# Loading the joint pass's constants and first tiles during the second feature transform

## The reference

```python
# second graph layer: one head, 2048 -> 768
h   = h1 @ W2                                  # "second transform"
e   = leaky_relu((h @ a_src)[src] + (h @ a_dst)[dst], 0.2)
ex  = exp(e - segment_max(e, dst)[dst])
gnn = segment_sum(h[src] * (ex / segment_sum(ex, dst)[dst]), dst) + b2

# linear attention, per head (12 heads of 64, 256 random features)
dash = q * 64 ** -0.25 @ proj.T                # proj: the random map
q_p  = exp(dash - diag(q) - max(dash)) + 1e-4
out  = (q_p @ context) / (q_p @ k_sum)         # context, k_sum: sums over the keys
mix  = out @ w_proj.T + b_proj

x = x + gnn + mix
```

## Time and profile before

| | before |
|---|---|
| median of three runs | 3599.15 us (3598.68 to 3605.56) |
| profiled execution: its time, its span | 3594.7 us, 3592.9 us |
| second transform, first issue to the last store's landing | 1761.6 to 2206.3 us |
| joint pass, first issue to last store's issue | 2208.0 to 2986.5 us |
| TensorE busy over the span | 3106.6 us (86%), mean granted clock 0.926 |
| DMA, whole span | 219 GB/s |

### The profile page before, as it was taken

The page is one execution under the profiler, slowest core; times in us unless marked ns, Lnnn a source line. Parts: engine busy times, 40 slices in busy tenths (PEclk is TensorE's granted clock), DMA queues, the critical chain, the costliest instruction groups (busy, mean ns, idle before and its releaser), DMA issues. The chain is left out here.

```text
span 3592.9 us, 63295 instructions
## 1 busy us (share of the span) xinstructions
PE 3106.6 (86%) x21962; PEld 2542.8 (71%) x21963; DVE 1944.3 (54%) x4537; ACT 1125.4 (31%) x2419; POOL 1503.7 (42%) x1497
## 2 busy tenths in 40 slices
PE   7974999999999789999799995999999996589920
PEld 6973677777777568889799995666666663389920
DVE  4853667666666554444522222666666664633357
ACT  2322434343434243333412221333333322223321
POOL 1323677777777400000000002777777751233346
PEclk9997999999999899999899997899999996689965
DMA  5746788888888465544466674999999975456767
GB/s 184 235 160 198 238 264 261 269 259 264 264 268 263 129 202 139 136 136 140 171 82 86 87 88 150 352 325 327 326 326 328 327 269 192 156 198 239 237 229 255
DMA packets 275948, 786.79 MB, mean 219 GB/s; under 512 B 81326, under 2 KB 94353, under 8 KB 272438
## 3 DMA queue, kind: packets, MB, share of 16 engines
q0 software_dynamic: 96640, 416.68, 35.5%
q1 hardware_dynamic: 178998, 366.17, 34.6%
HBM read 676.48 MB, written 167.42 MB: 235 GB/s over the span
## 5 line engine op out<-in xcount | busy, mean ns | idle before, releaser
L940 POOL DMA_INDIRECT k_rows<-tab,k_pick x576 | 598.1, 1038 | 234.7 <-issue 175.1
L2161 POOL DMA_INDIRECT m_rows<-tab,m_e x500 | 490.0, 980 | 200.8 <-issue 143.4
L1400 PE MATMUL k_num<-k_rows,k_wt 128*32 128x384 f32 (+1 forms) x3200 | 283.2, 494 | 14.3 <-ACT k_wt L1032 14.3
L142 PE MATMUL g_prod<-g_w_hi,g_h_h 128*128 128x384 f32 x768 | 258.0, 336 | 3.4 <-DVE g_h_l L1766 3.4
L143 PE MATMUL g_prod<-g_w_lo,g_h_h 128*128 128x384 f32 x768 | 257.8, 336 | 0.0
L144 PE MATMUL g_prod<-g_w_hi,g_h_l 128*128 128x384 f32 x768 | 257.8, 336 | 0.0
L1661 PE MATMUL f_prod<-f_a_h,f_w_hi 128*128 128x512 f32 (+1 forms) x672 | 253.9, 378 | 2.5 <-DVE f_w_lo L1604 2.5
L1663 PE MATMUL f_prod<-f_a_h,f_w_lo 128*128 128x512 f32 (+1 forms) x672 | 246.5, 367 | 0.0
L1662 PE MATMUL f_prod<-f_a_l,f_w_hi 128*128 128x512 f32 (+1 forms) x672 | 246.4, 367 | 0.0
L1730 POOL MEMSET g_row<- 128x1 f32 x2 | 0.1, 101 | 542.3 <-issue 542.3
L1597 DVE TENSOR_TENSOR f_a_l<-f_turn,f_a_h 128x512 fp32r<-128x512 f32 (+1 forms) x168 | 98.8, 628 | 210.1 <-ACT f_a_h L1564 210.1
(11 more groups left out here) (366 smaller groups left out, 7675.5 us busy)
## 6 DMA issues: line engine op xcount, KB each, us to landing
agg<-k_outb SPq DMA_DIRECT2D x100, 384.0 KB
f_a_in<-agg SPq DMA_DIRECT2D x100, 384.0 KB, 7.3
g_h<-h SPq DMA_DIRECT2D x25, 1024.0 KB, 12.1
ys<-e_y SPq DMA_DIRECT2D x56, 384.0 KB, 2.9
h<-f_e SPq DMA_DIRECT2D x16, 1024.0 KB, 5.2
tab<-q_xn SPq DMA_DIRECT2D x25, 388.5 KB, 5.4
tab<-g_row SPq DMA_DIRECT2D x25, 385.5 KB, 4.6
m_own<-tab SPq DMA_DIRECT2D x25, 385.5 KB, 9.0
```

Of the source, the lines that this page charges most:

```text
L142: pe.matmul(out, x_hi[k], w_hi[k], start=(k == 0), stop=False)
L940: pool.indirect_dma_start(rows[:, place(u, n), :], None, dram["tab1"], at, bounds_check=bound, oob_is_err=False).then_inc(rows_in[i], 16)
L1400: mm = pe.matmul(num[i][o, 0:n], wt[u % 2][:, v, o], rows[:, place(u, 2 * (half + v) + g), a:a + n], start=(v == 0), stop=(v == 1), tile_p ...
L2161: pool.indirect_dma_start(rows[:, place(h, c) + k, :], None, tab, bass.IndirectOffsetOnAxis(ap=e[h % 4][:, 0, k * SLOTS + c:k * SLOTS + c ...
```

## The change

A new class `QueryAhead` owns, in an outer pool around both stages, the buffers and semaphores of the map, the context, the diagonal, the projection weights, the low parts of the two query tiles and the four edge-list buffers. SyncE fills them inside the second transform, right after `store(1)`, once the last weight piece has been split; these are 24 DMAs: map (2), diagonal, context, query tiles 0 and 1, projection weights (6), edge lists of tiles 0, 1 and 2 (12). The staging ring of `W2` has no buffers of its own any more: it uses those of the projection weights and so has 12 places instead of 16. In the joint pass SyncE starts with the ramp, input tile 0 and the biases; in each turn the own rows now come first, then edge lists, query tile, input tile. The outer pool ends with a barrier of its own. In the skipped variant the same class is made inside its pool.

```diff
+class QueryAhead:
+    HELD = 3
+    def fetch(self, sp):
+        for i, buf in enumerate((self.pj_h, self.pj_l)):
+            sp.dma_start(buf[:, :].bitcast(F32), self.dram["pj"][i, :, :]).then_inc(self.pj_in, 16)
+        sp.dma_start(self.diag[:, :], self.dram["mix"][:, CTXW:MIXW]).then_inc(self.diag_in, 16)
+        sp.dma_start(self.ctx[:, :], self.dram["mix"][:, 0:CTXW]).then_inc(self.ctx_in, 16)
+        for t in range(2):
+            self.load_q(sp, t)
+        for k in range(KC):
+            sp.dma_start(self.w[:, k, :], self.io["wprojT"][k * P:(k + 1) * P, :]).then_inc(self.w_in, 16)
+        for h in range(self.HELD):
+            self.load_edges(sp, h)
...
-def phase_g(nc, io, dram, keep):
+def phase_g(nc, io, dram, keep, ahead):
...
-        SR = 16
-        stage = [s.sb(f"stage{b}", [P, 384]) for b in range(SR)]
+        SR = 2 * KC
+        stage = [ahead.w[:, b // 2, 384 * (b % 2):384 * (b % 2) + 384] for b in range(SR)]
...
                 sp.dma_start(dram["ald2"][bass.ds(r, P), :], row[b][:, D + 2:D + 3]).then_inc(out_sem[b], 16)
+                if first and b == 1:
+                    sp.wait_ge(wlo_done, len(JOBS))
+                    ahead.fetch(sp)
...
-                load_q(0)
-                for i, (buf, n) in enumerate(((pj_h, 0), (pj_l, 1))):
-                    sp.dma_start(buf[:, :].bitcast(F32), dram["pj"][n, :, :]).then_inc(pj_in, 16)
-                sp.dma_start(diag[:, :], dram["mix"][:, CTXW:MIXW]).then_inc(diag_in, 16)
+                if not merged:
+                    held.fetch(sp)
                 if merged:
                     sp.dma_start(ramp[:, :], io["node_ids"][0:P].partition_broadcast(P)).then_inc(ramp_in, 16)
-                    load_edges(0)
-                sp.dma_start(ctx[:, :], dram["mix"][:, 0:CTXW]).then_inc(ctx_in, 16)
+                load_x(0)
                 sp.dma_start(bias[:, :], io["bproj"].partition_broadcast(P)).then_inc(bias_in, 16)
                 if merged:
                     sp.dma_start(att[1][:, :], io["b2"].partition_broadcast(P)).then_inc(bias_in, 16)
-                load_x(0)
-                load_q(1)
-                if merged:
-                    load_edges(1)
                 for t in range(NT + 2):
-                    if merged and t + 2 < NT:
+                    if merged and t < NT:
+                        load_own(t)
+                    if merged and QueryAhead.HELD <= t + 2 < NT:
                         load_edges(t + 2)
                     if t + 2 < NT:
                         load_q(t + 2)
                     if t + 1 < NT:
                         load_x(t + 1)
-                    if merged and t < NT:
-                        load_own(t)
-                    if t == 0:
-                        for k in range(KC):
-                            sp.dma_start(w[:, k, :], io["wprojT"][k * P:(k + 1) * P, :]).then_inc(w_in, 16)
                     if t >= 2:
                         store(t - 2)
...
-        phase_g(nc, io, dram, keep)
-        mix_out(nc, io, dram, keep, True)
-        mix_out(nc, io, dram, keep, False)
+        with Pool(nc, "a") as a:
+            ahead = QueryAhead(nc, io, dram, keep, a)
+            phase_g(nc, io, dram, keep, ahead)
+            mix_out(nc, io, dram, keep, ahead)
+        mix_out(nc, io, dram, keep, None)
```

More of the change, by code:

```diff
@@ L1746, in _ @@
                 act.wait_ge(staged[n % SR], 16 * (n // SR + 1))
-                act.activation(w_hi[:, k, o], stage[n % SR][:, :], ACT.Copy).then_inc(whi_done, 1)
+                act.activation(w_hi[:, k, o], stage[n % SR], ACT.Copy).then_inc(whi_done, 1)
             def step(p, b, first, last):
@@ L2009, in _, with mix_out @@
                 groups(pe, lambda T: None, group, lambda T, n: None)
-def mix_out(nc, io, dram, keep, merged):
+def mix_out(nc, io, dram, keep, ahead):
+    merged = ahead is not None
     GR = P // TW
@@ L2025, in mix_out @@
     with Pool(nc, "m" if merged else "c") as s:
-        pj_h, pj_l = s.sb("pj_h", [P, M], F32R), s.sb("pj_l", [P, M], F32R)
-        ctx, diag = s.sb("ctx", [P, CTXW]), s.sb("diag", [P, NT * HEADS])
-        w = s.sb("w", [P, KC, D])
-        qt_h, qt_l = s.sb2("qt_h", [P, KC, P], F32R), s.sb2("qt_l", [P, KC, P], F32R)
+        held = ahead if merged else QueryAhead(nc, io, dram, keep, s)
+        pj_h, pj_l, ctx, diag, w, qt_l = held.pj_h, held.pj_l, held.ctx, held.diag, held.w, held.qt_l
+        qt_h = s.sb2("qt_h", [P, KC, P], F32R)
         qp, qpt = s.sb("qp", [P, HEADS * M]), s.sb2("qpt", [P, 4 * P])
@@ L2046, in mix_out @@
             ramp, ones = s.sb("ramp", [P, P]), s.sb("ones", [P, P])
-            e = [s.sb(f"e{b}", [P, 2, S], I32) for b in range(4)]
+            e, e_in = held.e, held.e_in
             rows = s.sb("rows", [P, RING, TROW2])
@@ L2057, in mix_out @@
             out_b = [s.bank(f"out{i}") for i in range(2)]
-            ramp_in, e_in = s.sem("ramp_in"), [s.sem(f"e_in{b}") for b in range(4)]
+            ramp_in = s.sem("ramp_in")
             ald_in, own_in, rows_in = s.sem2("ald_in"), s.sem2("own_in"), keep["rows_in"][1]
@@ L2081, in load_q @@
                         sp.wait_ge(dash_full, 6 * (t - 1))
[L2082 to L2083 removed]
+                    held.load_q(sp, t)
                 def load_x(t):
@@ L2092, in load_edges @@
                         sp.wait_ge(z1_done, h - 3)
-                    for k in range(GR):
-                        lo = sp.value_load(keep["ranges"][0:1, 2 * (GR * h + k):2 * (GR * h + k) + 1], min_val=0, max_val=EP)
-                        sp.dma_start(e[h % 4][:, :, k * SLOTS:(k + 1) * SLOTS],
-                                     io["edges"][:, bass.ds(lo, CAP)].rearrange("s (p c) -> p s c", c=SLOTS)).then_inc(e_in[h % 4], 16)
+                    held.load_edges(sp, h)
                 def load_own(h):
```

27 lines of the change are left out of this document (21 added, 6 removed).

## The result

| | before | changed |
|---|---|---|
| median, runs side by side | 3600.30 us (3598.68 to 3605.56) | 3662.54 us (3660.39 to 3663.52) |
| ratio, 95% interval | | 1.0169 [1.0152, 1.0187] |
| profiled execution: time, span | 3594.7, 3592.9 us | 3660.4, 3658.6 us |
| start of the second transform | 1761.6 | 1764.4 |
| second transform (to the first issue of the joint pass) | 446.4 us | 459.5 us (+13.1) |

The forecast was 3596 us in 3585 to 3606; the time lies far above the range. Of the 65.7 us between the two profiled executions 48.5 stand in the joint pass and 13.1 in the transform.

What follows compares the result with a forecast made beforehand. TensorE was taken to bound both stages, leaving gain only at their boundary. Boundary -12.5, fetch +8.0, staging ring +0.7, barrier +0.5 sum to -3.3 us: 3591.4 from the profiled execution, 3596 us as median, range 3585 to 3606.

Steps and rivals of the forecast that it cites:

- The input tile's landing: Joint-pass turn: input tile issued about 11 us later, lands 7.3 us after issue, in time for GpSimd; costs nothing.
- The rest: Outer pool's barrier, 0.5 us, and the new order of loads in each joint-pass turn, said to cost nothing.
- The second rival: Joint pass: input tile late in every turn; at a 12 us landing it costs 31 us, 3627 us; chance 0.08.
- The fetch's price: Second transform: fifth transposed tile's load, queued behind the fetch, lands 5.5 us late; with the clock 8.0 us, bounds 0 and 13.3.
- The clock's share: Second transform: after the pause at the fifth tile, some 6 us at half clock cost 2.5 us.
- The ring: Second transform: staging ring cut from 16 to 12 slots delays the second transposed tile, 0.7 us, between 0 and 2.0.
- The barrier: Outer pool: ten semaphores cleared in one more barrier, 0.5 us, between 0.3 and 1.
- The gain at the boundary: Joint pass's start: earlier loads gain 12.5 us, between 9.0 (gathers' lead) and 14.2 (products, maxima and exponentials).
- The sum: Both stages: boundary gain, fetch, staging ring and barrier together, -3.3 us.
- given back: Main case: start's gain partly lost again to a pause in the transform; 3589 to 3604 us, chance 0.60.
- No pause: Second transform: fetch costs nothing, sum -11.3 us, 3588 us, down to 3585; chance 0.26.

Runs made afterwards that it cites:

- f1: Changed kernel with the old order of loads in each joint-pass turn, fetch still in the transform: 3598.1 us, ratio 1.0008.
- f2: Kernel before with only the new order, own rows at the head of each joint-pass turn: 3649.6 us, ratio 1.0148.
- g1: Changed kernel with the input tile issued right behind the own rows, ahead of edge lists and query tile: 3600.1 us, ratio 1.0012.
- g4: Changed kernel with the finished tile's store moved to the head of each turn, nothing behind the input tile: 3745.5 us, ratio 1.0417.
- g3: Changed kernel with the old turn order and the second tile's column store replaced by one 512-byte row of other data: 3588.5 us, ratio 0.9982.
- f3: Changed kernel with only the input tile issued at the head of each turn, ahead of the own rows: 3600.7 us, ratio 1.0015.
- e5: Changed kernel with the old turn order and the fetch issued after the transform's last transposed-tile load: 3588.3 us, ratio 0.9979.
- e1: Changed kernel with the old order of loads in each turn, on a slower chip: 4071.9 us, ratio 1.0000.
- e3: Changed kernel with only the input tile issued at the head of each turn, on a slower chip: 4078.8 us, ratio 1.0025.
- f7: Changed kernel with the input tile issued right behind the own rows, on a slower chip: 4084.3 us, ratio 1.0027.
- f6: Changed kernel with the old turn order and the second tile's column store replaced by one 512-byte row, on a slower chip: ratio 0.9952.
- e2: Kernel before with only the new order, own rows at the head of each turn, on a slower chip: 4086.1 us, ratio 1.0027.

## Why the prediction was wrong, step by step

- **The input tile's landing, in "The rest": the step that failed.** The forecast put the new order at nothing. I moved the tile's issue by 11 us and took the landing of 7.3 us from the earlier trace rows, measured in another order. The budget was right: without its wait GpSimd would have added at 2344.85 - 4.37 = 2340.5, 7.9 us after the issue at 2332.5, against the 8.6 forecast. That tile was added to 12.3 us after its issue; the middle landing was 14.6. The turn grew by 31.70 - 29.34 = 2.4 us. Over the twenty turns from the fifth to the last addition, 47 us, GpSimd's waits for the tile come to 71.9 us and its waits for ring slots fall from 50.2 to 6.7: 1.4 us a turn. Most of the rest, 0.8 us a turn, stands in GpSimd's own instructions and the short gaps between them, 16.8 us longer in sum; why is open. So the slack was 2.5 us a turn, not the 2.00 of one wait, and it was used up. Against f1, which has the same start, 4.8 us more are lost before these turns and 2.8 behind them: 54.8 us in all, of which the start's gain hides 6.3. f1 and f2 show it from both sides. The second rival named this mechanism, its threshold of 10.6 us and the place; its price of 31 us was for a landing of 12 us. I gave it 0.08, since I read the landing as a property of the transfer. It goes with the order: own rows, four lists and the query tile are issued in the 6.4 us before it, the store right behind, all beside the gathers. g1 and g4 part this only roughly. Of the 15.4 us in the crowded start, which I had quoted, I should have asked what made it: there, too, the tile stands in a bunch. The Trainium skill (DMA: Bandwidth & Descriptors, section Queues, rings and completion order) says that each DMA engine takes the descriptors of one issuing engine in their order. The landings of 9.2 us with the own rows alone right ahead and 12.0 with the lists and the query tile between them agree with it; they don't show it by themselves.
- **The clock in the joint pass**, not in the forecast: TensorE was at half clock for 102.6 us in place of 67.8 (from the stage's mean granted clock, 0.939 and 0.957). It follows the waits (61 us in f1, 202 in g4), and so is part of what the late tile costs; how much of it no run separates.
- **The fetch's price, 8.0 us: mechanism right, size and place off.** One pause, at the fifth tile, as forecast, of 9.0 us in place of 5.5. The load went 29.1 us after the fetch's start, not 26.3, landed in 5.9 us, not 4.9, the fetch began 0.5 us later in the stage, and the tile was needed 0.8 us later: 5.5 + 2.8 + 1.0 + 0.5 - 0.8 = 9.0. The clock's share, 2.5 forecast: a window of 8 us after the pause shows 0.70, so 4.8 us at half, worth 2.4 at most. I had put the hold on the edge lists, by the earlier trace rows; it fell on the weight loads (9.45 us for six), and the lists went nearly unhindered (15.56 us, 14.2 counted). What held them was the column store, which I had named by its 33 GB/s in the earlier trace rows: g3 shows 5.6 us of issue and 6.8 us of the stage. The Trainium skill (DMA: Bandwidth & Descriptors, section Issuing engines are not separate DMA queues) calls the time to start a DMA usually small relative to the DMA itself. Here 12 lists of 5 KB took 15.56 us to issue, and in f1 and the changed kernel the tile behind the fetch paid.
- **The ring, 0.7 us (0 to 2):** the early pause grew by 5.24 - 3.39 = 1.9 us here, and by some 1.8 over all traces, so my value was low and the bound about right. In this pair part of it came back before the fifth tile, which was needed only 0.8 us later: after the early pause the clock was at half for 4.1 us in place of 6.0. So 9.0 + 2.4 + 0.8 = 12.2 us, and TensorE's last product of the transform does end 12.3 us later; the other 0.8 of the 13.1 stand behind it.
- **The barrier, 0.5 us (0.3 to 1):** some 1.4 us, above the bound, and in the joint pass's 839.9 us. I had read the 0.3 us between two semaphore instructions of the earlier trace rows and not what the engines do around them.
- **The gain at the boundary, 12.5 us (9.0 to 14.2):** first maximum 13.4 us early (14.2 forecast), first gather 8.1 (9.0), VectorE's wait at the second tile 2.16 (about 2 forecast). The rows' use came 9.5 us early, not 12.5: the last gather of that tile began at +56.6, only 7.8 us early, and its rows were used at +62.6, which is 5.0 us after its end, not 3. And it did not last: in f1 the third tile's rows are used 94.3 - 101.5 = 7.2 us early, and the stages of f1, f3, g1, g3 and e5 are 3.9 to 6.3 us shorter than before's 791.4, with the barrier of 1.4 in them. In f1's second tile the trace shows where some 2 us went: TensorE waits 3.10 us for the maxima, which wait for the gathered rows, and its clock falls for the stretch after:

```profile
2280.00:2290.00 10.00, 6.90 (x21) 4.17 (x21) 7.90 (x19) 2.26 (x4) 7.66 (x8) 0.66 0.99 343
```

```profile
2280.00:2290.00 10.00, 8.48 (x56) 6.17 (x52) 9.35 (x22) 3.18 (x7) 7.56 (x9) 1.00 0.96 345
```

  (first f1, then before, columns as in the earlier trace rows; in both the second tile's rows are used from 2280 on; 0.66 against 1.00.) So 12.5 should have been about 7, below the lower bound of 9.0. That bound took the gathers' lead to be kept in full; it was not.
- **Two slips that changed nothing:** twelve loads, not ten, stood ahead of the second query tile, and eleven lists at 2.2 in place of 1.2 us lose 11 us, not 12; the measured loss in issue was 29.1 - 19.6 = 9.5.
- **The sum** with what the changed kernel shows, the order left out: -7.2 + 11.4 + 0.8 + 1.4 = +6.4, against -3.3. With the 54.8 us of the order it gives 61.2 of the 61.6 us by which the two stages grew. The profiled f1, which has all of the change but the order and a shorter pause (7.2), took 3.7 us more in its two stages. Had the turn's order been left alone, the forecast's "given back" case would have stood: 1.0008. On the forecast's base that is 3602 us, inside its 3589 to 3604, though on the slower side of no change. "No pause" was wrong in the changed kernel, and e5 shows what it would have needed: the fetch where nothing urgent is queued behind it.

## What to carry to other kernels

A landing time read from a trace holds for the place in the queue where it was read. When a load is moved behind others, count the bytes issued in the microseconds ahead of it and take the landing of a load that already stands in such a bunch; if the slack is under that, order is the whole question. And an early fetch is paid by what is queued behind it, so its place is after the last urgent load (e5), not at the first moment when its buffers are free.

## What the runs showed of the hardware

- One store of 128 single numbers (512 bytes in all) ahead of large loads delays their issue: six weight loads in 7.33 to 9.54 us with it (changed kernel, f1, f3, g1, g4), 4.95 without it (g3); on the slower kind 7.37 to 8.48 (e1, e3, f7) and 3.69 (f6).
- The landing of a 384 KB load beside the gathers ran from 7.2 to 14.6 us in the middle with its place in the queue and in the turn (f1 7.2, g1 9.2, g4 12.0, changed kernel 14.6). What is issued ahead went with 5.4 us of it, what is behind with 2.6; how much is the moment among the gathers is open.
- One more all-engine barrier with a clear of semaphores took some 1.4 us (12.7 us in the mean between the joint pass's last store and the next stage without it, 14.2 with it).
- Chips differ in what they move for the same program. Table by stretch, 540 us of the settled joint pass of e1 (slower kind) and of before:

```profile
2560.00:3100.00 540.00, 436.37 (x2931) 276.52 (x2933) 256.72 (x568) 123.00 (x265) 284.49 (x276) 0.86 0.72 237
```

```profile
2340.00:2880.00 540.00, 505.30 (x4035) 331.94 (x4032) 354.03 (x784) 171.34 (x368) 395.73 (x388) 1.00 0.93 327
```

  Both the share and the rate are lower, 0.72 and 237 GB/s, and the clock is 0.86. The second transform, which has no gathers, took as long on either kind (445.8 us in e2 and in f2). What limits such a chip stays open. With turns of 40 us the order of the loads hardly mattered: e2's ratio was 1.0027 where f2's was 1.0148. A change that lives on 2 us of slack must be measured where the slack exists.
